# ScalarE takes the sums, squares and scaling of x for the first five feed-forward blocks

## What is computed

```python
def _L0_ffn_ref(x, ...):
    h = x
    for blk in range(3):
        i0, i1 = (2 * blk, 2 * blk + 1)
        y = _qlora_linear(h, ...i0)
        y = _layernorm(y, ln_gamma[blk], ln_beta[blk])
        y = jax.nn.gelu(y, approximate=False)
        y = _qlora_linear(y, ...i1)
        h = y + h
    return h
x = x + _L0_xattn_ref(ctx_1024, ctx_1024, _layernorm(x, axis=-1), ...)
x = x + _L0_ffn_ref(_layernorm(x, axis=-1), ...)
```

## Time and profile before

| | us |
|---|---|
| median of 3 runs | 377.6 (377.5 to 378.43) |
| the profiled execution | 380.3 |
| its span, first to last instruction | 378.5 |
| PE busy | 340.5 (90%) |
| DVE busy | 330.5 (87%) |
| ACT busy | 289.5 (76%) |
| POOL busy | 267.6 (71%) |

### The profile page before, as it was taken

The page is one execution under the profiler, slowest core; times in us unless marked ns, Lnnn a source line. Parts: engine busy times, 40 slices in busy tenths (PEclk is TensorE's granted clock), DMA queues, the critical chain, the costliest instruction groups (busy, mean ns, idle before and its releaser), DMA issues.

```text
span 378.5 us, 12988 instructions
## 1 busy us (share of the span) xinstructions
PE 340.5 (90%) x4772; PEld 253.0 (67%) x4772; DVE 330.5 (87%) x826; ACT 289.5 (76%) x577; POOL 267.6 (71%) x264
## 2 busy tenths in 40 slices
PE   3766899999999999999979786889999999999984
PEld 2343556776677667766756564776788888888863
DVE  6437999999999999999998999869999999988752
ACT  7646887888788878887866554557989999999862
POOL 6321988788788877887887878967778778774321
PEclk9979999999999999999998999899999999999999
DMA  5593764685467546854651400000001001100112
GB/s 156 152 286 111 216 212 141 192 248 168 142 190 237 176 138 197 237 168 145 202 196 53 145 2 2 3 2 0 3 29 58 28 28 38 48 29 29 55 43 71
DMA packets 53122, 43.29 MB, mean 114 GB/s; under 512 B 4496, under 2 KB 46944, under 8 KB 53088
## 3 DMA queue, kind: packets, MB, share of 16 engines
q1 hardware_dynamic: 53088, 42.84, 37.7%
HBM read 26.05 MB, written 16.78 MB: 113 GB/s over the span
## 4 chain that ended last, share of the span: by engine, by line
PE 60%; DVE 21%; issue 8%; ACT 4%; POOL 3%; DMA 2%; SPq 1%; POOLq 0%; DVEq 0%; ACTq 0%
PE score_ps L1240 9%; PE att_ps L1216 7%; PE score_ps L1159 6%; PE wo_ps L1031 5%; DVE zsum L694 5%; DVE negmax L680 5%; PE score_ps L1043 3%; PE work L1067 3%; DVE st L717 3%; PE work L1301 3%; PE score_ps L1308 3%; PE score_ps L1234 2%; PE att_ps L1308 2%; PE work L1073 2%; PE work L1080 2%
## 5 line engine op out<-in xcount | busy, mean ns | idle before, releaser
L444 POOL TENSOR_TENSOR probs<-probs,rz 128x1024 f32<-128x1024 f32 x64 | 136.2, 2140 | 40.7 <-DVE rz L697 40.5
L455 POOL TENSOR_TENSOR rs<-ve,minus_half 128x4 f32<-128x4 f32 (+1 forms) x50 | 59.4, 1187 | 43.1 <-DVE ve L633 31.7
L882 ACT ACTIVATE probs<-score_ps 128x1024 f32<-128x1024 f32 x64 | 65.6, 1025 | 26.0 <-PE score_ps L1159 25.6
L680 DVE TENSOR_REDUCE negmax<-score_ps 128x64 bf16<-128x1024 f32 x64 | 75.2, 1175 | 4.8 <-PE score_ps L1043 4.7
L694 DVE TENSOR_REDUCE zsum<-probs 128x64 f32<-128x1024 f32 x64 | 77.3, 1208 | 1.6 <-ACT probs L882 1.6
L930 ACT ACTIVATE z<-score_ps,rs 128x128 f32<-128x128 f32 x160 | 46.0, 384 | 2.8 <-POOL rs L455 2.8
L1159 PE MATMUL score_ps<-negmax,ident_bf 128*128 128x512 bf16 x128 | 39.2, 388 | 9.7 <-DVE negmax L680 9.6
L1240 PEld LDWEIGHTS score_ps<-lin_t,h 128*128 128x128 f32 x320 | 39.0, 192 | 12.6 <-DVE h L755 7.7
L1031 PEld LDWEIGHTS wo_ps<-wo_t,att_t 128*128 128x128 f32 x256 | 37.3, 193 | 13.7 <-issue 12.1
L1240 PE MATMUL score_ps<-lin_t,h 128*128 128x128 f32 x320 | 42.3, 280 | 3.3 <-ACT probs L882 1.1
L1216 PE MATMUL att_ps<-probs,v_diag 128*32 128x64 f32 x2048 | 43.4, 225 | 1.6 <-POOL probs L444 1.4
(11 more groups left out here) (184 smaller groups left out, 672.2 us busy)
## 6 DMA issues: line engine op xcount, KB each, us to landing
q_parts<-parts SPq DMA_DIRECT2D x16, 512.0 KB, 3.5
k_stack<-k_parts SPq DMA_DIRECT2D x32, 256.0 KB, 3.4
q_stack<-q_parts SPq DMA_DIRECT2D x64, 128.0 KB, 2.9
ctx_sb<-in_ctx SPq DMA_DIRECT2D x16, 256.0 KB, 3.7
k_parts<-parts SPq DMA_DIRECT2D x16, 256.0 KB, 2.9
out<-x_all SPq DMA_DIRECT2D x16, 256.0 KB, 2.3
x_all<-in_x SPq DMA_DIRECT2D x14, 256.0 KB, 3.8
x_all<-in_x SPq DMA_DIRECT2D x1, 512.0 KB, 4.9
```

The source lines that it names most:

```text
L444: nc.gpsimd.tensor_tensor(e[:, :, :, :], e[:, :, :, :], by_query.broadcast_to([P, BANDS, SEQ, ADJ]), ALU.mult).then_inc(s_probs, 1)
L455: nc.gpsimd.tensor_tensor(rs2[v][:, lo:hi], ve2[v][:, lo:hi], minus_half[:, lo:hi], ALU.pow).then_inc(p_rs[v], 1)
L680: nc.vector.tensor_reduce(negmax[p % 2][:, :], score_ps[p % 2][:, :].rearrange("p (h k) -> p k h", k=SEQ), AX_X, ALU.max, negate=True).the ...
L882: nc.scalar.activation(probs[p][:, :, :, :], score_ps[p % 2][:, :].rearrange("p (u s k) -> p u k s", s=ADJ, k=SEQ), ACT.Exp, scale=SCALE). ...
```

## The change

For blocks 0 to 4 ("the first five") the statistics of x, and the writing of `z[0]`, leave DVE and POOL for ACT. Four tables say where the new pieces stand: `MEANS`, `SQUARES` and `SCALED` in ACT's chunks, `SCALES` in POOL's. In `input_means` ACT runs four copies of x scaled by -1/128 into a buffer that nobody reads (`junk`), for their sums along the features, which are the negated means `nm2`. In `input_squares` it runs four Square instructions with `nm2` as bias, for the sums of the squared distances (`xsq2`). POOL's `input_scales` makes the scale and `nmr2` of it in three small instructions. In `input_scaled` ACT writes `z[0]` in four instructions, with the scale and `nmr2` as operands. `nm2`, `xsq2`, `rs2` and `nmr2` exist once, so each piece waits for the readers of the block before; these waits are in the diff. DVE has nothing left of steps 0 and 1, and only the first layer's half of `combine_input` in steps 2 to 4. From step 5 on everything is as before; counts in the waits are shifted.

```diff
 EARLY = {"PE": {0: (12, 3), 1: (13, 3), 2: (15, 0), 4: (16, 2)},
-         "DVE": {0: (12, 3), 1: (13, 3), 2: (15, 1), 3: (16, 0), 4: (16, 3)},
-         "ACT": {0: (12, 3), 1: (13, 3), 2: (15, 2), 3: (15, 3), 4: (16, 2)},
-         "POOL": {0: (12, 3), 1: (13, 3), 2: (15, 1), 3: (16, 0), 4: (16, 2)}}
+         "DVE": {2: (15, 1), 3: (16, 0), 4: (16, 3)},
+         "ACT": {1: (13, 3), 2: (15, 2), 3: (15, 3), 4: (16, 2)},
+         "POOL": {2: (15, 1), 3: (16, 0), 4: (16, 2)}}
 FIRST_STEP = 5
+
+MEANS = {0: (12, 2), 1: (14, 0), 2: (14, 2), 3: (15, 0), 4: (15, 2)}
+SQUARES = {0: (12, 3), 1: (14, 1), 2: (14, 3), 3: (15, 1), 4: (15, 3)}
+SCALES = {0: (13, 0), 1: (14, 2), 2: (15, 0), 3: (15, 2), 4: (16, 0)}
+SCALED = {0: (13, 1), 1: (14, 3), 2: (15, 1), 3: (15, 3), 4: (16, 1)}
...
+            def input_scales(t):
+                pool.wait_ge(p_xsq, t + 1)
+                if t > 0:
+                    pool.wait_ge(p_xrs, t)
+                nc.gpsimd.tensor_scalar(ve2[1][:, 0:TPC], xsq2[:, :], 1.0 / D, EPS, ALU.mult,
+                                        ALU.add).then_inc(p_xst, 1)
+                pool.wait_ge(p_xst, t + 1)
+                if t > 0:
+                    pool.wait_ge(p_z[0], t)
+                nc.gpsimd.tensor_tensor(rs2[1][:, 0:TPC], ve2[1][:, 0:TPC], minus_half[:, 0:TPC],
+                                        ALU.pow).then_inc(p_xrs, 1)
+                pool.wait_ge(p_xrs, t + 1)
+                nc.gpsimd.tensor_tensor(nmr2[:, :], nm2[:, :], rs2[1][:, 0:TPC], ALU.mult).then_inc(p_nmr, 1)
...
             def step(t, par):
-                if isinstance(t, int) and t <= FIRST_STEP:
-                    dve.wait_ge(s_x2, t + 1 if t < FIRST_STEP else NCHUNK)
-
-                if live(t) and isinstance(t, int) and t <= FIRST_STEP:
-                    ins = input_stats(t)
-                    if t < 2:
-                        ins.then_inc(p_bn[1], 1)
+                if isinstance(t, int) and t == FIRST_STEP:
+                    dve.wait_ge(s_x2, NCHUNK)
+                    input_stats(t)
...
+                input_part(SCALED, c, 0, input_scaled)
+                input_part(SQUARES, c, 0, input_squares)
+                input_part(MEANS, c, 0, input_means)
                 early_steps("ACT", c, 0, step)
...
+            def input_means(t):
+
+                act.wait_ge(s_x2, t + 1)
+                if t > 0:
+                    act.wait_ge(p_nmr, t)
+                    act.wait_ge(p_xmean, t)
+                for i in range(TPC):
+                    ins = nc.scalar.activation(junk[:, 0, i, :], x_all[:, t, i, :], ACT.Copy, scale=-1.0 / D,
+                                               accum_out=nm2[:, i:i + 1])
+                ins.then_inc(p_xmean, 1)
+
+            def input_squares(t):
+
+                act.wait_ge(p_xmean, t + 1)
+                if t > 0:
+                    act.wait_ge(p_xst, t)
+                    act.wait_ge(p_xsq, t)
+                for i in range(TPC):
+                    ins = nc.scalar.activation(junk[:, 1, i, :], x_all[:, t, i, :], ACT.Square, bias=nm2[:, i:i + 1],
+                                               accum_out=xsq2[:, i:i + 1])
+                ins.then_inc(p_xsq, 1)
+
+            def input_scaled(t):
+
+                act.wait_ge(p_nmr, t + 1)
+                if t > 1:
+                    act.wait_ge(p_zt[0], t - 1)
+                for i in range(TPC):
+                    ins = nc.scalar.activation(z[0][t % 2][:, i, :], x_all[:, t, i, :], ACT.Identity,
+                                               bias=nmr2[:, i:i + 1], scale=rs2[1][:, i:i + 1])
+                ins.then_inc(p_z[0], 1)
```

More of the change, by code:

```diff
@@ L236, in live, with later @@
             return not isinstance(c, int) or 0 <= c < NCHUNK
+        def later(t):
+            return not isinstance(t, int) or FIRST_STEP <= t < NCHUNK
         def some(count):
@@ L255, in early_steps, with input_part @@
                         step(t, t % 2)
+        def input_part(places, c, p, part):
+            if isinstance(c, int):
+                for t, place in places.items():
+                    if place == (c, p):
+                        part(t)
         def chunks(eng, body):
@@ L638, in combine_input @@
                 st, ag = st2[1][:, lo:hi, :], ag2[1][:, :, lo:hi]
-                dve.wait_ge(p_bn[1], k + 1)
-                if some(k):
-                    dve.wait_ge(p_rs[1], k)
+                dve.wait_ge(p_bn[1], k - 1)
+                if some(k - 2):
+                    dve.wait_ge(p_rs[1], k - 2)
                 nc.vector.scalar_tensor_tensor(ag[:, 1, :], st[:, :, 2], EPS * D, st[:, :, 5], ALU.add, ALU.add)
@@ L645, in combine_input @@
                 nc.vector.tensor_tensor(ag[:, 2, :], st[:, :, 1], st[:, :, 4], ALU.subtract).then_inc(p_mv[1], 1)
-                dve.wait_ge(p_mv[1], 2 * k + 1)
+                dve.wait_ge(p_mv[1], 2 * k - 3)
                 if lo == 0:
-                    if some(k):
-                        dve.wait_ge(p_nmr, k)
+                    dve.wait_ge(p_nmr, k)
                     nc.vector.tensor_scalar(nm2[:, :], ag[:, 0, 0:TPC], -0.5, None, ALU.mult)
@@ L738, in step @@
                     layer_stats(1, TPC, first_layer_bank(1, t, par)).then_inc(p_bn[1], 1)
-                if live(t) or live(t - 2):
-                    combine_input(t, 0 if live(t) else TPC, 2 * TPC if live(t - 2) else TPC)
+                if live(t - 2):
+                    combine_input(t, 0 if later(t) else TPC, 2 * TPC)
                 if not isinstance(t, int) or (t >= FIRST_STEP and live(t + 1)):
@@ L897, in chunk @@
                     q_low(c + 2, par)
+                input_part(SCALED, c, 1, input_scaled)
+                input_part(SQUARES, c, 1, input_squares)
+                input_part(MEANS, c, 1, input_means)
                 early_steps("ACT", c, 1, step)
```

27 lines of the change are left out of this document (20 added, 7 removed).

## The result

The change makes the kernel slower. The median goes from 377.55 to 390.3 us (four runs each, 388.15 to 391.42 with it), a ratio of 1.032 with a 95% interval of 1.028 to 1.036. The profiled execution of the changed kernel took 388.15 us, its span 386.3, 7.85 us more than the profiled execution of before. So the forecast for that one execution (387.8, span 386.0) came out close, and the forecast for the median (385.1, range 381.0 to 389.5) is 5.2 us short, and 0.8 us outside its range. Both have to be explained: where 7.85 us come from, and why the medians lie 12.75 apart.

The account below looks back on a forecast made before the run. Bound by a chain from DVE instruction to DVE instruction in chunks 12 to 15, then along PE. GELU 7.0 us late plus 0.5 for the clock, 7.5 on the median of 377.6, gave 385.1 us; range 381 to 389.5.

Parts of the forecast that it names:

- the queue laid out again: Chunks 12 to 15 up to step 5: start of each exponential on the old trace's clock; GELU 7.0 us late.
- the wait: Chunk 14: ACT's means of block 2 wait 3.5 us for POOL's `nmr` of block 1.
- The price of a read: ACT's means and squares: reading the accumulator adds 0.08 us to each instruction.
- case C: Slower still: a read costs 0.18 us, clock loss 2 instead of 0.5, 389.1 us; one end of the forecast's 0.86.
- D: Free accumulator reads and no clock loss, 381.9 us; the other end of the forecast's 0.86.
- Rival B: No change: POOL is early and ACT's waits do not bite; without 7.0 us of waiting 378.1 us; chance 0.05.
- point 7: Chunk 15: DVE's queue, with step 2's remainder at 1.5 us, and POOL's product put `nmr` at 239.0, (15,3) 5.1 late.
- the second wait: Part (15,2): ACT's means of block 4 wait 2.8 us for POOL's `nmr` of block 3.
- point 2: Chunk 13: (13,0) to (13,1) 2.1 us at full clock for 4.04; (13,2) at 205.5 for 206.03.
- point 4: Chunk 14, means and squares of block 1: (14,2) at 217.4 for 219.17, the last gain, 1.8 us.
- the clock term: PE behind its longer idle times: lower clock can lose up to 2 us behind the GELU; 0.5 us added.
- Rival A: Faster: ACT's new groups fit into its gaps and hide everything, 5.5 us gained, 372.1 us; chance 0.07.

Follow-up runs that it names:

- the second tile: Changed kernel with the sums (means) of the first five blocks going to two small tiles in turn instead of one; 382.7 us, ratio 1.011.
- scales first: Changed kernel, single tile, with POOL's three scale operations moved ahead of the product of the probabilities; 385.5 us, ratio 1.021.
- filled kernel before: Kernel before with 18 matmuls by zeros added to PE where it stood idle, nothing left out; 377.3 and 377.2 us, ratio 0.998 both times.
- 63 zeros: Changed kernel with 63 matmuls by zeros added to PE ahead of its waits, nothing left out; 388.2 us, ratio 1.024.

## Why the prediction was right and wrong

**Right: the chain through the change-over.** Against the profiled execution the points of the queue laid out again came out so (predicted, measured): (13,0) 198.5, 198.37; (13,1) 200.6, 200.53; (13,2) 205.5, 205.56; (14,0) 212.4, 212.35; (14,1) 214.4, 214.51; (14,2) 217.4, 217.45; the wait 3.5, 3.37; (14,3) 222.9, 223.02; (15,0) 228.1, 228.34; (15,1) 230.8, 231.23. (12,3) was at 193.41 for 193.6. The price of a read, 0.08 us from the nearest row, was 0.10, so case C (0.18) and D (nothing) are both out. My estimate of 0.09 from the fixed time and the overlap in the Trainium skill (ScalarE: Activation LUTs, section "What ACT_TABLE_LOAD costs") agrees with the rows. The Trainium skill's rule for VectorE, that an accumulator output makes two instructions (VectorE: DVE Perf Modes, section "Two Vector instructions with no wait between them"), holds for ScalarE in this trace, where the read has a row of 0.19 us.

**Right: the wait, and its price.** Rival B took 7.0 us of waiting out of the sum; the second tile took out 7.6 by the medians and 6.7 by the profiles, scales first 4.8.

**Mis-sized: DVE's remainder of step 2** in point 7, 1.5 us. It took 2.7, from 231.12 to 233.82:

```profile
231.12 0.82 DVE L753 BATCH_NORM_STATS2 st<-work 128x6 f32<-128x128 f32 x4
231.98 1.45 DVE L679 SCALAR_TENSOR_TENSOR ag<-st 128x4 f32<-128x4 f32 x1
...
233.82 1.22 DVE L716 TENSOR_REDUCE negmax<-score_ps 128x64 bf16<-128x1024 f32 x1
```

```profile
231.28 2.12 POOL L463 TENSOR_TENSOR probs<-probs,rz 128x1024 f32<-128x1024 f32 x1 [1.32 <-DVE rz L733]
```

An instruction on 4 columns took 1.45 us, and ended when POOL's product did (233.40); of the twelve of this line between 200 and 330 us the median is 0.17. In the kernel before the same instruction of step 0 took 1.69 us at 194.05 and also ended with a product of POOL; the prediction did not carry that row over. The Trainium skill (SBUF — State Buffer, section "Who interferes with whom") says that a DVE instruction with two inputs in SBUF contends with a GpSimd instruction that reads SBUF, for a lock that one of them holds alone; both rows agree with that. With it `nmr` of block 3 ended at 240.50 for 239.0 (1.2 us of the remainder, and 0.2 by which the sum of (15,0) began late), the second wait was 3.4 for 2.8, and (15,3) was 1.5 and the GELU 1.6 us later than predicted. From there on 13.0 us passed to step 5 for my 14.0 (the 13.5 of before and 0.5 for the clock), which gave 1.0 us back. That the profiled execution came out at 388.15 for 387.8 is therefore in part luck: 1.6 and -1.0 nearly cancel, and it was the one profile of three in which the half clock cost nothing.

**Wrong: the step to the median,** "the same 7.5 us on the median of 377.6". The profiled execution of before (380.3) had half clock at 197 to 201 and 238 to 242. In point 2 I put (13,0) to (13,1) at 2.1 us for 4.04 "at full clock" and booked the difference as a gain of the change. In the filled kernel before the same distance is 3.0 us, so more than half of that gain was the clock of one execution. The ends of the stretch in the two filled kernels, before and then changed with 63 zeros:

```profile
188.52 1.02 ACT L886 ACTIVATE probs<-score_ps 128x1024 f32<-128x1024 f32 x1
...
191.49 1.02 ACT L886 ACTIVATE probs<-score_ps 128x1024 f32<-128x1024 f32 x1 [0.20 <-PE score_ps L1170]
...
249.93 1.16 PE L1251 MATMUL score_ps<-lin_t,h 128*128 128x128 f32 x8 [0.78 <-DVE x_all L705]
```

```profile
189.81 1.03 ACT L918 ACTIVATE probs<-score_ps 128x1024 f32<-128x1024 f32 x1
...
193.65 1.01 ACT L918 ACTIVATE probs<-score_ps 128x1024 f32<-128x1024 f32 x1
...
262.02 1.16 PE L1327 MATMUL score_ps<-lin_t,h 128*128 128x128 f32 x8 [0.78 <-DVE x_all L741]
```

(14,2) comes 28.0 us after (12,2) in the filled kernel before, not the 29.3 of the profile, and 27.9 with the change: of the gain of 1.8 in point 4, 0.1 is left at full clock. In full, 63.8 - 61.4 = 2.4 us of before's profile were not in its median, so the change costs 72.2 - 61.4 = 10.8 us at full clock, where the two profiles show 8.4. The medians of the filled kernels say the same, 388.2 - 377.3 = 10.9.

**Mis-sized: the clock term,** 0.5 us for a loss between 0 and 2. In two profiles of three of the changed kernel it was 3.1 to 3.3, half of it at 199 to 203, a stretch in which I had looked for none: PE's idle time there had moved from DVE's maximum to ACT's exponential and had not gone (2.08 and 1.69 us). The Trainium skill (TensorE: Matmul & The Clock Gate, Part 1) says that idleness throttles the array; the prediction had called 2 us the likelier for it and put 0.5, and both were too small for these two profiles. The median lost less than they did, 390.3 - 388.2 = 2.1 us against the runs with 63 zeros. 10.9 + 2.1 = 13.0, for 12.75 between the medians.

**Rival A** was wrong in size as well: with everything hidden I put 372.1 us, 5.5 us of gain, and 2.6 were measured with nearly all of ACT's work left out.

## What to carry to other kernels

Work moved to an engine that looks half idle is not free where the engine's own instructions are links in the chain (of some 20 us of new work on ScalarE 6.9 reached the end even without the wait), and a buffer that exists once ties it to the slowest reader's place in another queue: lay out the queues, and give the buffer a second tile first. Ask what the move can give with its work at no cost (here 2.6 us of 378) before pricing it. And before a sum made on one profiled execution is put on a median, compare the two; where the profiled one is longer, look for stretches at 1.2 GHz and make the sum without them.
